# A graph-network kernel: counts built one node tile later, small chains moved beside products, and another order with a second filter buffer in the message stage

## The reference

```
for l in range(3):                       # layer 1
    neigh = segment_sum(h[src], dst) / max(deg, 1)
    h = h @ Ws_self[l] + neigh @ Ws_neigh[l] + bs[l]     # relu but for the last
x = layernorm(x + h)

s, v = (xs @ w_in_s)[idx_j], (xv @ w_in_v)[idx_j]        # layer 2, idx_i = src, idx_j = dst
W = (ssp(f_ij @ W1 + b1) @ W2 + b2) * rcut_ij            # ssp(x) = softplus(x) - log 2
edge = [s*y0*W0, (v.yv)*IS3*W1, s*yv*W2, v*y0*W3, ...]   # the further parts reach no output
agg = segment_sum(edge, idx_i)
out = ssp(agg_s @ w_f2o1_s) @ w_f2o2_s ,  agg_v @ w_f2o1_v @ w_f2o2_v
x = layernorm(x + out)
```

## Time and profile before

| | us |
|---|---|
| median of 3 runs | 2094.54 (2092.11 to 2095.12) |
| the profiled execution's own time | 2094.46 |
| its span | 2092.6 |
| PE busy | 1906.2 (91%) |
| DVE busy | 1289.1 (62%) |
| POOL busy | 1079.9 (52%) |
| ACT busy | 594.7 (28%) |
| mean granted clock of PE | 0.956 of full |

### The profile page before, as it was taken

One profiled execution on the slowest core, in us unless ns is written; L12 is line 12 of the kernel. 1 busy time (PEld: TensorE's weight loads), 2 busy tenths in 40 slices (PEclk: granted clock), 3 DMA queues, 4 the chain that ended last, 5 costly groups with the idle time before them and its releaser, 6 DMA issues. The chain is left out here.

```text
span 2092.6 us, 23699 instructions
## 1 busy us (share of the span) xinstructions
PE 1906.2 (91%) x8445; PEld 1216.9 (58%) x8445; DVE 1289.1 (62%) x1985; ACT 594.7 (28%) x1380; POOL 1079.9 (52%) x1054
## 2 busy tenths in 40 slices
PE   7799999999999999999999999999837778888886
PEld 3344455555555555555555566666635567676775
DVE  6899989677763343333333355555325688878785
ACT  1355532100000000000000001111225566676773
POOL 4000000000047888788887874288777777666660
PEclk9899999999999999999999999999869899999997
DMA  4255444322223333333322247356423333232330
GB/s 141 65 176 187 172 153 167 117 87 88 88 85 95 99 111 101 106 94 95 95 94 80 74 158 243 116 187 208 141 91 99 114 88 109 82 98 81 98 91 20
DMA packets 111705, 240.15 MB, mean 115 GB/s; under 512 B 28358, under 2 KB 51811, under 8 KB 111584
## 3 DMA queue, kind: packets, MB, share of 16 engines
q1 hardware_dynamic: 77008, 179.10, 26.2%
q0 software_dynamic: 34576, 59.48, 10.2%
HBM read 163.76 MB, written 74.72 MB: 114 GB/s over the span
## 5 line engine op out<-in xcount | busy, mean ns | idle before, releaser
L1057 PE MATMUL low<-table,abuf 125*125 125x512 f16 x3750 | 844.0, 380 | 4.8 <-DVE abuf L1497 4.8
L1057 PEld LDWEIGHTS low<-table,abuf 125*125 125x125 bf16 x3750 | 505.3, 137 | 300.4 <-issue 28.0
L901 PE MATMUL mid<-wbuf,h_t 128*125 128x512 f32 x1200 | 560.0, 603 | 5.4 <-DVE st_out L1539 3.8
L789 POOL DMA_INDIRECT by_src<-scat_row,sort x416 | 490.0, 1178 | 126.1 <-issue 118.8
L794 POOL DMA_INDIRECT table<-msg_table,wbuf x300 | 317.8, 1059 | 137.3 <-issue 82.5
L1091 PE MATMUL low<-table,wbuf 128*125 128x256 f32 x900 | 255.5, 443 | 121.8 <-DVE table L1785 121.8
L901 PEld LDWEIGHTS mid<-wbuf,h_t 128*125 128x125 f32 x1200 | 215.1, 190 | 210.5 <-issue 200.4
L781 POOL TENSOR_TENSOR scat_row<-scat_row 128x64 f32<-128x64 f32 x26 | 16.0, 617 | 558.1 <-DVE sort L1659 557.5
L1091 PEld LDWEIGHTS low<-table,wbuf 128*125 128x125 f32 x900 | 196.1, 221 | 171.1 <-DVE table L1785 132.3
L1497 DVE TENSOR_TENSOR abuf<-abuf,row_scale 125x3125 bf16<-125x3125 bf16 (+3 forms) x84 | 256.5, 3059 | 3.4 <-DMA abuf<-adj 3.4
L1546 DVE SCALAR_TENSOR_TENSOR y<-low,inv_deg,st_in 125x512 f32<-125x512 f32 x75 | 56.3, 750 | 328.1 <-PE low L1057 210.9
(11 more groups left out here) (210 smaller groups left out, 1717.3 us busy)
## 6 DMA issues: line engine op xcount, KB each, us to landing
abuf<-adj SPq DMA_DIRECT2D x75, 781.2 KB, 4.7
adj<-table SPq DMA_DIRECT2D x25, 781.2 KB, 4.6
states<-st_out SPq DMA_DIRECT2D x75, 256.0 KB, 2.0
st_in<-states SPq DMA_DIRECT2D x75, 256.0 KB, 4.7
early_rows<-sort POOLq DMA_DIRECT2D x25, 384.0 KB, 3.0
table<-early_rows SPq DMA_DIRECT2D x25, 384.0 KB, 6.0
by_src<-scat_row,sort POOLq DMA_INDIRECT x416, 2.2
by_src<-blank SPq DMA_DIRECT2D x25, 252.0 KB, 4.4
```

The costliest lines, as they stand in the source:

```text
L789: pool.indirect_dma_start(out=by_src, out_offset=bass.IndirectOffsetOnAxis(ap=place_i[:, k * PIECE + j:k * PIECE + j + 1], axis=0), in_=sc ...
L901: last = pe.matmul(to[0:TN, :], h_t[i % 2][:, k, :], weights[l % 2][:, a, k, :], start=k == 0, stop=k == KC - 1)
L1057: last = pe.matmul(p_agg[k % 2][0:TN, :], a_tile[k % 3][:, a, :], table[ps % 2][0:TN, a, h, :], start=a == 0 and h == 0, stop=a == TILES - ...
```

## The change

`LAG` is 7: the tiles of counts are built one node tile later, their first one-hots at w = 6 and their last at k = 5. The trip of the degrees on SP moves from w = 4 to w = 5 (L625), where `store_state(4)` stands ahead of it, and PE's `transpose_codes` goes from behind the products of w = 4 to before those of w = 5. `degrees_and_rounds` is split into `rounds` (w = 5) and `mean_factors` (w = 6). `row_scales(0)` and `row_lo(0)` stand before `first_edges`. Bins are placed four per round in k = 9 to 15, with `bin_starts` at k = 8, and the places end at k = 16. Two `adj` stores inside the loop over further count planes are widened; that loop runs only where an edge count or a run is too large.

In the message stage `filt_h` gets a second buffer, and three orders change: PE's `output_1(t-1)` comes before `sums(t, 2)`, ACT's `output_1(t-1)` comes at the end of round t rather than early in round t+1, and ACT's `root(t-1)` comes before `scaled(t, 2)`.

```diff
--- before.py
+++ after.py
@@ -43,7 +43,7 @@
 RUN = P + 1
 PER_BANK = 4
 PARTS = -(-BLOCKS // PER_BANK)
-LAG = 6
+LAG = 7
 CHUNK = NODES * TN
 A_ROW = TILES * TN + 11
 
@@ -249,7 +249,7 @@
     wreg = Region(wbuf[:, :, :].rearrange("p a k -> p (a k)"), 2 * 2 * KC * D * 4)
     m_relu = wreg.take(P, [NBLK, P])
     m_exp = wreg.take(P, [NBLK, P])
-    filt_h = wreg.take(P, [NBLK, P])
+    filt_h = [wreg.take(P, [NBLK, P]) for _ in range(2)]
     feat_t = wreg.take(P, [NBLK, P])
     hot32 = wreg.take(P, [SLOTS, TN])
     win_p = [wreg.take(P, [SLOTS, PAY]) for _ in range(3)]
@@ -572,8 +572,8 @@
                 sp.dma_start(g_dst[:, :], dst[0:P * CH].rearrange("(p c) -> p c", p=P)).then_inc(s_gl, 16)
                 sp.wait_ge(s_gdone, q)
                 for plane in range(2):
-                    sp.dma_start(adj[bass.ds(q + ((plane + 1) * TILES - 1), 1), 0:TN, :].rearrange("a p k -> (a p) k"),
-                                 bt[plane].rearrange("p a d -> p (a d)")).then_inc(s_gst, 16)
+                    sp.dma_start(adj[bass.ds(q + ((plane + 1) * TILES - 1), 1), :, :].rearrange("a p k -> (a p) k"),
+                                 bt_wide[plane]).then_inc(s_gst, 16)
                 wait_alone(sp, s_gst, q * 32 + 1)
 
             def far_planes(ps):
@@ -622,7 +622,7 @@
                         sp.wait_ge(s_iota, IOTAS)
                     for to, of in later[(w - 8) * 2:(w - 7) * 2]:
                         sp.dma_start(to, of).then_inc(s_const, 16)
-                if w == 4:
+                if w == LAG - 2:
                     sp.wait_ge(s_degn, 1)
                     sp.dma_start(bass.AP(degrees.tensor, 0, [[NODES, EP], [NODES * EP, GB], [1, NODES]]), node_deg[:, :, :]).then_inc(s_degst, 16)
                     sp.wait_ge(s_degst, 16)
@@ -659,7 +659,7 @@
                     t = k - 8
                     sp.dma_start(blank_sums[t, :, :], zeros[:, 0:2 * N * G // (P * TILES)]).then_inc(s_zero, 16)
                     sp.dma_start(blank_rows[t, :, :], zeros[:, 0:N * G // (P * TILES)]).then_inc(s_zero, 16)
-                if k == 9:
+                if k == 10:
                     sp.wait_ge(s_count, 1)
                     extras(sp, blank_extra_window)
                     sp.sem_inc(s_filled, 1)
@@ -1013,10 +1013,10 @@
                     if tb is not None and step < PARTS:
                         multiply_blocks(tb, step)
 
+                if w == LAG - 2:
+                    transpose_codes()
                 product(w, 0, blocks_between)
                 product(w, 1, blocks_between)
-                if w == LAG - 2:
-                    transpose_codes()
 
             for k in range(AGGS):
                 ps, i = k // TILES, k + TILES - 1
@@ -1038,7 +1038,7 @@
                             message_product(i)
                     if tb is not None and a in BLOCKS_AT:
                         multiply_blocks(tb, BLOCKS_AT.index(a))
-                    if k == 6 and a == 8:
+                    if k == LAG and a == 4:
                         bin_sums()
                     if k == 61 and a == 4:
                         pe.wait_ge(s_emax, 1)
@@ -1077,7 +1077,7 @@
                 pe.wait_ge(s_mh, t + 1)
                 if n >= 2:
                     pe.wait_ge(s_w_free, n - 1)
-                filter_products(p_w[n % 2], [filt_h[0:BLK * F + 1, GS // BLK * g + b, :] for b in range(GS // BLK)], CUTS).then_inc(s_w2, 1)
+                filter_products(p_w[n % 2], [filt_h[t % 2][0:BLK * F + 1, GS // BLK * g + b, :] for b in range(GS // BLK)], CUTS).then_inc(s_w2, 1)
 
             def sums(t, g):
                 n = t * NG + g
@@ -1153,9 +1153,9 @@
                     features(t + 2)
                 if t + 1 < TILES:
                     filters(t + 1, 0)
-                sums(t, 2)
                 if t >= 1:
                     output_1(t - 1)
+                sums(t, 2)
             output_2(TILES - 2)
             for step in (output_t, output_1, output_2):
                 step(TILES - 1)
@@ -1329,8 +1329,6 @@
             hots(0)
             for t in range(TILES):
                 scaled(t, 0)
-                if t >= 2:
-                    output_1(t - 2)
                 if t + 1 < TILES:
                     hidden(t + 1)
                 scaled(t, 1)
@@ -1338,12 +1336,13 @@
                     hots(t + 1)
                 if t >= 1:
                     output_t(t - 1)
+                if t >= 2:
+                    root(t - 1, s_ovar, s_orstd)
                 scaled(t, 2)
                 if t + 2 < TILES:
                     features(t + 2)
-                if t >= 2:
-                    root(t - 1, s_ovar, s_orstd)
-            output_1(TILES - 2)
+                if t >= 1:
+                    output_1(t - 1)
             root(TILES - 1, s_ovar, s_orstd)
             output_t(TILES - 1)
             output_1(TILES - 1)
@@ -1411,11 +1410,13 @@
                                           node_iota32[0:EP, 0:NODES].unsqueeze(1).unsqueeze(3).broadcast_to([EP, GB, NODES, P]), ALU.is_equal))
                 dve.tensor_reduce(node_deg[:, :, :], in_node[:, :, :, :], AX.X, ALU.add).then_inc(s_degn, 1)
 
-            def degrees_and_rounds():
+            def rounds():
                 dve.wait_ge(s_ctp[1], 1)
                 ch.link(dve.tensor_scalar(flags[0:1, 3:4], p_b[1][0:1, 0:1], 1.0, float(TILES), ALU.min, ALU.mult))
                 ch.link(dve.tensor_scalar(rounds_i[0:1, 1:2], flags[0:1, 3:4], 1.0, None, ALU.add))
                 dve.sem_inc(s_meta, 1)
+
+            def mean_factors():
                 dve.wait_ge(s_degt, 1)
                 ch.link(dve.tensor_scalar(deg_t[0:TN, :], p_b[1][0:TN, 0:TILES], 1.0, None, ALU.max))
                 ch.link(dve.reciprocal(inv_deg[0:TN, :], deg_t[0:TN, :]))
@@ -1660,15 +1661,17 @@
 
             def hidden(t):
                 dve.wait_ge(s_mact, 3 * t + 3)
-                if t:
-                    dve.wait_ge(s_w2, NG * t)
-                dve.scalar_tensor_tensor(out=filt_h[0:BLK * F, :, :], in0=m_exp[0:BLK * F, :, :], scalar=-LOG2,
+                if t >= 2:
+                    dve.wait_ge(s_w2, NG * (t - 1))
+                dve.scalar_tensor_tensor(out=filt_h[t % 2][0:BLK * F, :, :], in0=m_exp[0:BLK * F, :, :], scalar=-LOG2,
                                          in1=m_relu[0:BLK * F, :, :], op0=ALU.add, op1=ALU.add).then_inc(s_mh, 1)
 
             chunks()
             for w in range(TILES):
+                if w == LAG - 2:
+                    rounds()
                 if w == LAG - 1:
-                    degrees_and_rounds()
+                    mean_factors()
                     general(dve, general_counts)
                     dve.wait_ge(s_cols, 4)
                 if builder_of(w + 1) is not None:
@@ -1677,11 +1680,11 @@
                 if w == TILES - 1:
                     scale(0, 0)
                     scale(0, 1)
+                row_scales(w)
+                row_lo(w)
                 if w == 0:
                     first_edges()
                     dve.wait_ge(s_bias, 16)
-                row_scales(w)
-                row_lo(w)
                 own_part(w)
                 if w == 2:
                     codes_first()
@@ -1702,11 +1705,11 @@
                     one_hot_codes(builder_of(TILES + k + 1))
                 if k > 2 * TILES:
                     normed(k - 1)
-                if k == 7:
+                if k == LAG + 1:
                     bin_starts()
-                if 8 <= k < 17:
-                    place_bins(range((k - 8) * 3, min(BINS, (k - 8) * 3 + 2)))
-                if k == 17:
+                if 9 <= k < 16:
+                    place_bins(range((k - 9) * 4, min(BINS, (k - 9) * 4 + 2)))
+                if k == 16:
                     places_last()
                 if k and i < AGGS:
                     row_scales(i)
@@ -1731,9 +1734,9 @@
                     far_planes(ps)
                 if ps == 2:
                     add_residual(k)
-                if 8 <= k < 17:
-                    place_bins(range((k - 8) * 3 + 2, min(BINS, (k - 7) * 3)))
-                if k == 16:
+                if 9 <= k < 16:
+                    place_bins(range((k - 9) * 4 + 2, min(BINS, (k - 8) * 4)))
+                if k == 15:
                     places_first()
                 if k == 60:
                     early_max()
@@ -1741,7 +1744,8 @@
                     early_need()
                 if k == 2 * TILES + 2:
                     dve.wait_ge(s_ps, AGGS)
-                    dve.memset(filt_h[BLK * F:BLK * F + 1, :, :], 1.0)
+                    for b in range(2):
+                        dve.memset(filt_h[b][BLK * F:BLK * F + 1, :, :], 1.0)
                 if k == AGGS - 1:
                     hidden(0)
             mean_plus_state(AGGS - 1)
```

## The result

The changed kernel takes 2025.8 us (median of four runs, 2022.36 to 2028.38) against 2094.74 (four runs, 2092.11 to 2095.12): a ratio of 0.967, 95% interval 0.966 to 0.969. The forecast was 2021, its range 2012 to 2056. The profiled execution is the fastest of the four, 2022.36, with a span of 2020.5; by its own span the kernel gained 72.1 us. The forecast's sum, made the same way, was 74.1.

A forecast was written before the change was run, and what follows sets the result against it. It saw message rounds bound by a loop through PE, ACT and DVE, closed by the single `filt_h`. -66.3 - 4.6 - 6.0 + 1.5 + 1.3 = -74.1 from 2094.5 gives 2020.4, plus 0.6 for ties: 2021, range 2012 to 2056.

The forecast's parts named there:

- Message stage: Rounds from `sums(5, 2)` to `sums(24, 2)`: 18 of 16.6 us and a last of 15.7, 314.5 against 380.8: -66.3 us.
- three engines meet at 16.5 to 16.7: Message-stage round: DVE without its waits, PE's tie with it before group 1, and POOL's 12 gathers all give about 16.6 us.
- Tail: After `sums(24, 2)`: `output_2(23)` follows 2.6 us after its start instead of 7.2, since `output_1(23)` is done before: -4.6 us.
- First pass: First 25 tiles: with `LAG` 7, tile 6's one-hots start at 74.8 instead of 81.09; taken as -6.0 us.
- the estimate of the degree store, 65.3: First pass: the degrees' store is issued at 65.3 rather than 61.43, 3.9 us later, so the first one-hots start at 74.8.
- Aggregation: Aggregation passes: the moved count tile's small matmuls cost PE +1.5 us, placing four bins per round +1.3.
- A: Message stage: the clock still falls before `sums(t, 2)`; rounds of 18.4 us, 2056 in all; chance 0.09.
- B: Message stage: POOL becomes the bound, its gathers stretched by a denser DVE; rounds of 17.9 us, 2045; chance 0.06.
- C: Message stage: ACT's queue behind `output_1(t-1)` makes `output_t` late and the kernel slower; rounds of 21.0 us, 2106; chance 0.02.
- D: Message stage: the double buffer brings little, since gathers come just in time; rounds of 18.7 us, 2060; chance 0.06.

The follow-up runs named there:

- orders only: Kernel before with the new PE and ACT orders and one filter buffer: 2058.26 us, ratio 0.983, on a quiet chip; an earlier disturbed run gave 1.003, no verdict.
- buffer only: Kernel before with the second `filt_h` buffer alone, old orders kept: ratio 0.997 (0.993 to 1.001), on a chip with `remote` waits, so no measure.
- eleven gathers: Kernel after without the last gather of group 2 from tile 2 on, so POOL has 11 a round instead of 12: 2022.06 us.

## Why the prediction was right, and where it was not

- **Message stage**, forecast -66.3, measured -65.4. Rounds 16.6 forecast, 16.60 measured; no wait of `hidden` or `output_scalars`; `output_1` on PE 1.7 us ahead of `sums(t, 2)`; clock 1.00. The statement that three engines meet at 16.5 to 16.7 held for DVE and POOL. PE's 15.9 was given as it is. The orders alone give 1.7 us a round and the buffer 1.85 more once they are there, 3.5 together; the share of the buffer alone stays open.
- **Tail**, forecast -4.6, measured -5.5 (24.67 us from `sums(24, 2)` to the end before, 19.1 after). `output_2` follows after 2.70 us, 2.6 forecast, which makes 4.5 of it. The other 0.9 the sum left out: the last `output_1` ran at the upper clock, 1.16 us in place of 2.07. This trace was a lucky one. After waits of 1.6 to 2.0 us, `sums(24, 2)` took 4.54 us in four of the kernels built from this one, and six of them needed 19.2 to 21.8 us from there to the end.
- **First pass**, forecast -6.0, measured -1.6 (-1.3 between the means of the traces that share a first pass). This is the step that failed: "`rounds` and `transpose_codes` move beside products that wait anyway: 0". Of the transposes on PE that is true, but their eviction on ACT, `columns`, moved as well, behind `row_hi(4)`, which waits 12.05 us for DVE. PE waits 6.52 us for it before product 5, and that product then runs at the lower clock. Undoing it gave 2.2 us back, 3.1 against the mean of the six traces. The other part is the estimate of the degree store, 65.3, which came at 66.96 even then, and a trip from there to the one-hots of 10.4 us against 9.5 (61.43 to 70.91): 1.7 + 0.9 = 2.6, from 74.8 to 77.3. `row_scales(0)`, forecast 0 with +1 as a bound, costs about 1.
- **Aggregation**, forecast +1.5 and +1.3, together +2.8; measured +0.4, since the first aggregation product starts 1.57 us earlier and `sums(5, 2)` only 1.18 earlier. The first transpose of `y` comes 2.8 us earlier than before (289.00 against 291.78), that of round k = 7 1.3 earlier (408.05, 409.35), that of k = 16 0.4 later (572.52, 572.15): +1.5 for the moved count tile and +1.7 for the placing. Both terms were right in kind, and the second is a little larger. What the sum had not are two gains. In the first round the lower clock ended sooner: its granted clock was 0.91 in place of 0.85, worth 1.2 us. And 1.6 came between the end of pass 1 and `sums(5, 2)`, 0.9 of it where PE waits for DVE's first normed tile (L881, 1.39 us in place of 2.27, at 1212 us). Why they came is not shown.
- **Rivals.** A: PE's wait fell to 0.7 to 1.6 us and the clock never fell in these rounds. B: a gather took 1.072 us on the mean in 1720 to 1980 us, 1.070 before, though DVE went from 82% busy to 98%. POOL was one of the engines that set the pace, as B had it, but at 16.6 and not at 17.9: the mean of 1.19 belongs to pass 2. The basis of B, the Trainium skill's rule on the shared port ("SBUF — State Buffer", Who interferes with whom), also names DVE instructions with two inputs in SBUF, which contend with a GpSimd instruction that reads SBUF. The trace agrees. Of the 189 gathers of the kernel after in that window 64 start inside one of the long DVE instructions with two such inputs (L1762, L1779, L1789), and 61 of these are stretched, to 1.15 us and more; of the 125 that start elsewhere none is. The stretched ones end 0.89 to 0.92 us after DVE leaves that instruction, and an undisturbed one takes 0.94. In pass 2 the stretched gathers are few and long: 14 of 120, up to 4.1 us, and 11 of them start inside DVE's 3.40 us `scale` (L1497), which has two such inputs too. So a gather's length depends on which DVE instruction it starts in and not on DVE's busy share, and of the 16.6 us of POOL's round about 1.5 are DVE's making, an estimate from 12 gathers of 1.072 in place of 0.94. C: ACT's queue was in time, with waits of 0.3 to 1.1 us only. D: the buffer does matter, once the orders are there.

The forecast of 2021 lay 4.8 us under the median; the profiled execution is itself 3.4 under that median. Against the traces the sum of -74.1 was 2.0 too large, and that it was no more is in part luck: the first pass fell short by 4.4 and the message stage by 0.9, while the aggregation gave 2.4 and the tail 0.9 that I had not counted on.

## What to carry to other kernels

When a loop through several engines is closed by more than one wait, list all the links before you price an edit: here half of the gain came only with the second edit, so such edits are tested together and then undone one at a time. Before you read a round from a trace, look for waits that the kernel cannot account for; behind one of them every later wait of the round is moved. After a gain, ask which engines are now full, and take load off each alone and off both: a chain of waits names one engine of a tie. When a short product is moved, follow its eviction into the queue of the engine that does it. Where equal programs scatter by 2 us, compare all traces that share the stage, not two.

## What the runs showed that I had not expected

The clock of `sums(t, 2)` against the wait before it, from round 6 on. Waits of 0.68 to 1.6 us (the kernel after, all rounds): 2.85 us, full clock, each time. 0.8 to 1.7 us (PE's order undone): full clock in all but one, which took 4.54 after a wait of 1.64. 1.9 to 2.2 us (orders only, but for the last two rounds): 2.85 in about half of the rounds, 4.1 to 4.5 in the others, in near alternation. 2.8 to 3.4 (before): lower clock in nearly all, and yet one 2.85. In buffer only it is `sums(t, 1)` that waits 2.1 to 2.4 us, and it took 4.4 to 4.5 in all 14 rounds. The same wait can go both ways, and so can equal rounds of two kernels: `sums(24, 2)` took 2.85 us after 1.61 in the kernel after and 4.54 after 1.62 with eleven gathers. So neither kernel can be priced with one value between. And the mean length of a gather, 1.055 to 1.100 us over five kernels in which DVE was busy between 82% and 98%, hides two lengths that the DVE instruction at its start decides.
